# A graph kernel on one core: which engine's queue carries the stores of running sums in layers 2 and 3

## The reference, cut to what matters

```
for l in range(3):                       # gated graph layers
    m   = x @ weight[l]
    agg = segment_sum(m[src] * edge_weight[:, None], dst, 6250)
    x   = gru_cell(agg, x, ...)
x = layernorm(x0 + x)
for W, b in ...:                         # three more layers
    x = relu((x + segment_sum(x[src], dst, 6250)) @ W.T + b)
x = layernorm(x1 + x)
```

## Time and profile before

| what | value |
|---|---|
| median of 3 runs | 2888.23 us (2887.8 to 2888.54) |
| the profiled execution's own time | 2885.88 us |
| its span, first to last instruction | 2884.1 us |
| granted TensorE clock, mean | 0.993 |
| PE busy | 2832.0 us, 98% |
| DVE busy | 1250.6 us, 43% |
| ACT busy | 946.7 us, 33% |
| POOL busy | 887.9 us, 31% |

### The profile page before, as it was taken

One profiled execution on the slowest core, in us unless ns is written; L12 is line 12 of the kernel. 1 busy time (PEld: TensorE's weight loads), 2 busy tenths in 40 slices (PEclk: granted clock), 3 DMA queues, 4 the chain that ended last, 5 costly groups with the idle time before them and its releaser, 6 DMA issues.

```text
span 2884.1 us, 72504 instructions
## 1 busy us (share of the span) xinstructions
PE 2832.0 (98%) x29387; PEld 1880.8 (65%) x29387; DVE 1250.6 (43%) x2716; ACT 946.7 (33%) x1891; POOL 887.9 (31%) x1007
## 2 busy tenths in 40 slices
PE   6899999999999999999999999999999999999998
PEld 5899999999999965555555555555655555555554
DVE  7688888777888514344422344343500010001011
ACT  6677777777777610000001011101400010001111
POOL 4244444444444315454541454544100000000000
PEclk8999999999999999999999999999999999999999
DMA  5666666666662299998996988988488868886884
GB/s 197 244 261 262 245 244 262 261 257 241 252 262 114 96 405 347 341 335 338 356 366 255 343 335 329 360 332 324 150 325 301 310 248 302 308 304 247 318 304 161
DMA packets 134009, 810.64 MB, mean 281 GB/s; under 512 B 17208, under 2 KB 27308, under 8 KB 113948
## 3 DMA queue, kind: packets, MB, share of 16 engines
q1 hardware_dynamic: 111228, 758.32, 68.2%
q0 software_dynamic: 19968, 40.46, 4.3%
q10 hardware_dynamic: 2720, 10.62, 0.9%
HBM read 553.01 MB, written 256.33 MB: 281 GB/s over the span
## 4 chain that ended last, share of the span: by engine, by line
PE 97%; ACT 1%; DVE 1%; DMA 1%; issue 1%; POOL 0%; DVEq 0%; POOLq 0%; ACTq 0%
PE ps L969 31%; PE ps L1165 27%; PE ps L1247 19%; PE ps L1240 11%; PE ps L979 1%; PE ps L980 1%; PE ps L1260 1%; PE ps L1261 1%; PE ps L982 1%; PE ps L981 1%; PE ps L1144 1%; ACT ring L1661 1%; DMA x_keep<-xT 0%; PE ps L1267 0%; PE ps L1266 0%
## 5 line engine op out<-in xcount | busy, mean ns | idle before, releaser
L969 PE MATMUL ps<-ring,Y 128*128 128x448 f32 x2352 | 888.4, 539 | 0.0
L1165 PE MATMUL ps<-ring,Y 128*128 128x448 f16 x4116 | 780.6, 352 | 0.0
L1661 ACT ACTIVATE ring<-ps 128x490 f16<-128x490 f32 (+1 forms) x1344 | 698.1, 653 | 182.8 <-PE ps L1240 175.5
L969 PEld LDWEIGHTS ps<-ring,Y 128*128 128x128 f32 x2352 | 446.4, 190 | 434.8 <-issue 434.8
L1165 PEld LDWEIGHTS ps<-ring,Y 128*128 128x128 f16 x4116 | 402.8, 98 | 373.8
L863 POOL DMA_INDIRECT ring<-y_rows,ring x448 | 431.6, 963 | 518.0 <-PE ps L969 261.8
L1247 PE MATMUL ps<-ring,Y 128*128 (+1 forms) x2744 | 571.8, 360 | 0.4 <-ACT shared L1620 0.4
L1247 PEld LDWEIGHTS ps<-ring,Y 128*128 128x128 f32 x2744 | 504.8, 190 | 8.7 <-ACT shared L1620 0.8
L1240 PEld LDWEIGHTS ps<-shared 64*128 64x128 bf16 x18816 | 320.0, 93 | 83.5 <-issue 65.4
L1240 PE MATMUL ps<-shared 64*128 64x49 bf16 (+1 forms) x18816 | 345.6, 189 | 24.2 <-DVE shared L2142 15.5
L1824 DVE TENSOR_SCALAR ring<-ring 128x128 f32<-128x128 f32 x446 | 130.6, 293 | 389.5 <-DMA ring<-y_rows,ring 254.2
(11 more groups left out here) (196 smaller groups left out, 1449.6 us busy)
## 6 DMA issues: line engine op xcount, KB each, us to landing
ring<-adj_w SPq DMA_DIRECT2D x72, 2688.0 KB, 11.9
ring<-adj_h SPq DMA_DIRECT2D x42, 2800.0 KB, 9.4
ring<-adj_h SPq DMA_DIRECT2D x42, 2688.0 KB, 9.3
adj_w<-ring SPq DMA_DIRECT2D x48, 2016.0 KB, 11.8
adj_h<-ring SPq DMA_DIRECT2D x56, 1372.0 KB, 5.0
ring<-adj_w SPq DMA_DIRECT2D x24, 2912.0 KB, 10.3
adj_w<-ring SPq DMA_DIRECT2D x48, 728.0 KB, 6.8
sum_rows<-ring SPq DMA_DIRECT2D x62, 448.0 KB
```

The source lines that it names most:

```text
L969: mm = pe.matmul(ps[:, bank, 0:GW], Y[:, h, :], slab(s)[:, :, h - h0, :], start=(h == 0), stop=(last and h == TILES - 1))
L1165: mm = pe.matmul(ps[:, par, 0:GW], part[:, h, :], counts_slab(par, s)[:, :, h - h0, :], start=(h == 0 and part is Y_high), stop=(h == TILE ...
L1661: act.activation(strip[:, :, c0:c0 + UNIT * WIN].rearrange("p h (d j) -> p d h j", d=WIN)[:, :, :, w0:w1], psum_unit(a)[:, :, kind, :, :]. ...
```

## The change

Stores 0 to 30 leave SyncE's stream; SyncE issues slabs only. GpSimd issues store b after the gather of round 7b + 12, that is, the sixth gather after the store's own last round, once `s_acc` shows that the seven rounds are summed. Store 31 stays where it was, but counts on the same semaphore as the others (`s_last` goes away), and the counts that DVE and GpSimd wait for are changed to match.

```
+STORE_LAG = 5
...
-            def store_sums(layer, b):
-                sp.wait_ge(s_acc, RUN * layer + STORE * (b + 1))
-                sp.dma_start(sums_kept(b), sums_made(b)).then_inc(s_stored[b % 2], 16)
...
                     for s in range(SLABS):
                         dense_slab(layer, g, s)
-                        if g or layer:
-                            for b in sums_due(SLABS * (g - 1 if g else DENSE - 1) + s):
-                                store_sums(layer if g else layer - 1, b)
...
                         stream_counts(0, 0, r, s)
-                        for b in sums_due(SLABS * (DENSE - 1) + HALVES * r + s):
-                            store_sums(N_LAYERS - 2, b)
...
                         .then_inc(s_row[i % ROW_BUFS], 16)
+                    if i % STORE == STORE_LAG and i > STORE:
+                        store_sums(layer, i // STORE - 1)
+
+            def store_sums(layer, b):
+                pool.wait_ge(s_acc, RUN * layer + STORE * (b + 1))
+                pool.dma_start(sums_kept(b), sums_made(b)).then_inc(s_stored[b % 2], 16)
 
             def fetch_ends(layer):
-                pool.wait_ge(s_acc, RUN * (layer + 1))
-                pool.dma_start(sums_kept(STORES - 1), sums_made(STORES - 1)).then_inc(s_last, 16)
-                pool.wait_ge(s_last, 16 * (layer + 1))
+                store_sums(layer, STORES - 1)
                 for half in range(2):
-                    pool.wait_ge(s_stored[half], 16 * (STORES // 2 - half) * (layer + 1))
+                    pool.wait_ge(s_stored[half], 16 * STORES // 2 * (layer + 1))
...
-                        dve.wait_ge(s_stored[half], 16 * ((STORES // 2 - half) * layer + store // 2))
+                        dve.wait_ge(s_stored[half], 16 * (STORES // 2 * layer + store // 2))
```

More of the change, by code:

```diff
@@ L351, in gnn_program @@
         s_ends = [sem(f"s_ends{i}") for i in range(RUN_SPANS)]
-        s_last = sem("s_last")
         s_joined = sem("s_joined")
@@ L550, in dense_slab @@
                 sp.dma_start(slab(s).rearrange("p u h c -> p (u h c)"), group_slab(g, s)).then_inc(s_slab[s], 16)
-            def store_sums(layer, b):
-                sp.wait_ge(s_acc, RUN * layer + STORE * (b + 1))
-                sp.dma_start(sums_kept(b), sums_made(b)).then_inc(s_stored[b % 2], 16)
-            def sums_due(slab_used):
-                return [b for b in range(STORES - 1) if max(PACE_FIRST + PACE_SLABS * STORE * (b + 1) // PACE, 0) == slab_used]
             def dense_streams(layer, first=0):
```

## The result

The changed kernel takes 2895.51 us (2893.17 to 2905.22, 8 runs) against 2888.14 us for the kernel before: ratio 1.0029, 95% interval 1.0019 to 1.0038. It is 0.3% slower where 2889.0 us, no change, was forecast. Its profiled execution took 2894.24 us, span 2892.5 us, 8.4 us more than before.

What follows compares the result with a forecast made beforehand. TensorE was taken to bound the kernel, fully busy in both layers' aggregations, so idle time elsewhere was worth nothing. Terms 0 + 0 + 0 + 0.8 + 0 = +0.8 us on 2888.23 gave 2889.0 us, range 2885.2 to 2896.

Steps and rivals of the forecast that it cites:

- SyncE's stores and DVE's wait: Two terms: slabs asked for up to 4.9 us sooner, and most of DVE's 134.6 us store wait going; each worth 0.
- the wait moved and nothing else: Rival on DVE: the 134.6 us on stores come back as waits on gathers; time as forecast, no chance of its own.
- GpSimd's issue and its wait for rows: GpSimd along each layer: 31 more stores at 0.9 us and a tighter wait, hidden in the pace; worth 0.
- The pace rival: Along both layers: typical landings of 12.2 us make seven rounds outlast the pace, backlog 19 us a layer, 2926 us; chance 0.03.
- The end of a layer: Layer 2's end: store 30 delays round 223 and store 31 by 3.3 us, of which +0.8 arrives; bounds 0 and 10.6.
- slower by the last stores: Rival at round 223's gather: store 30 holds it 7.8 us, +7.8 in layer 2, +5.9 in layer 3, 2901.9 us; chance 0.14.
- Layer 3: Layer 3's end: round 223 and store 31 1.5 us later, less than the 1.94 us before mix 10; worth 0.
- The range: Whole kernel's time: 2885.2 us (all that PE misses) to 2896 us (one layer end paying the last-stores rival's 7.8 us).
- slower: Whole kernel slower by over 0.2% (5.8 us): chance 0.14, from 0.11 for late last stores and 0.03 for pace.

Runs made afterwards that it cites:

- e17: Changed kernel, with TensorE doing the matmuls of layer 2's first flip four times over (24 more): 2896.82 us, ratio 1.0035.
- e11: Changed kernel with STORE_LAG 2 instead of 5, each store behind three further gathers, not six: 2927.71 us, ratio 1.0138.
- e3: Changed kernel, with SyncE loading the residual after layer 3's first four slabs instead of before them: 2888.55 us, ratio 1.0003.
- e13: Changed kernel with the rounds of both layers one slab (10.3 us) earlier: 2887.34 us, ratio 1.0000 to the kernel before.
- e1: Changed kernel again, unedited, as a yardstick: 2896.23 us, ratio 1.0028 to the kernel before.
- e12: Changed kernel again, unedited, as reference on the chip of its runs: 2895.65 us, ratio 1.0029 to the kernel before.
- e5: Changed kernel with only layer 2's stores on GpSimd's queue, layer 3's back on SyncE's: 2897.80 us, ratio 1.0042.
- e18: Kernel before with only layer 2's store 30 moved to GpSimd's queue, plus 24 added matmuls at layer 2's first flip: 2895.05 us, ratio 1.0026.
- e7: Changed kernel with STORE_LAG 6 (store 30 behind round 223) and the residual's load behind layer 3's first four slabs: 2887.74 us, ratio 1.0005.
- e2: Changed kernel with STORE_LAG 6 instead of 5, so store 30 comes behind the gather of round 223: 2890.32 us, ratio 1.0010.
- e16: Kernel before with eight plain transfers of gather size added behind layer 2's end gathers on GpSimd's queue: 2885.81 us, ratio 0.9997.
- e15: Kernel before with eight more gathers behind layer 2's end gathers and the first flip's matmuls repeated 16 times: 2899.05 us, ratio 1.0042.

## Why the prediction was wrong

*SyncE's stores and DVE's wait: 0 and 0.* Right. PE is 456.00 of 456 us busy, DVE's 134.6 us went and the wait for rows rose by 116 us, for nothing. In e17, the changed kernel with added matmuls in a trace of the same kind as that of before, the wait for rows is 396.9 us, against 254.2 + 134.6 = 388.8 for both before: the wait moved and nothing else, as that rival said.

*GpSimd's issue and its wait for rows: 0.* Right, with the condition: at six gathers the waits are 75.3 us over 20, hidden in the pace but for the last; at three (e11) they are 281.9 over 61 and the gap at layer 2's end is 18 us wider. The pace rival's way was right, its point of decision lies further off.

*The end of a layer: +0.8 us.* This is the step that failed, and twice.

First its size. I let store 30 hold round 223 back by 0.9 + 2.4 us. The 2.4 us were the landing of a store beside the residual's load less that of end gathers issued ten microseconds later, beside other loads. Measured: 0.6 us of issue and 14.3 - 9.1 = 5.2 us of landing, 5.8 in all. The residual's load, which the prediction mentions beside rows 8, has no term in its sum. SyncE issues it 3 us before GpSimd issues store 30:

```profile
1473.43 0.33 SPq L618 DMA_DIRECT2D shared<-x_keep  x1
```

e3 and e13, which take it away from store 30 and round 223, bring the landing to 8.2 and 7.5 us. The trace's packet records show how: the store has 4 packets of 7168 bytes per engine, which begin 1.2 us apart, each turn holding a packet of 25088 bytes of the residual's load, 0.93 us long; in e3 they begin 0.3 us apart. 4 x 0.93 = 3.7 us is most of the 5.2. The Trainium skill says in "DMA: Bandwidth & Descriptors", "Queues, rings and completion order", that an engine takes turns between its queues and goes on to the next only when a whole packet is done. This trace agrees: each of the store's packets ahead of the gather cost a whole packet of the load.

Second, the absorption. I had 3.3 us shrink to 0.8 because later end gathers would land faster. They were issued 5.9 us late and the gap grew by 5.5 in this trace, by 7.7 and 7.3 in e1 and e12: nothing was absorbed. There was a cliff where I drew a slope. With gathers still under way at the slab's end TensorE's own semaphore comes late (4.03, 5.61, 5.53 us in three traces), it idles, and its clock falls to 0.50 for the gates; or, if the semaphore is in time, the next slab's transfer gets in the way of the last gathers (e5, e17, e18). The rival "slower by the last stores" named the right place; its price for layer 2, 7.8 us, is about what the medians show (7.4 to 8.0 us), and I gave it 0.14.

*Layer 3: 0.* Right in the end: 506.24 us from its first aggregation to its flip in both traces. The delay of 1.5 us that I expected did not come: measured from layer 3's first aggregation, store 31 was issued 0.4 us earlier than before (2010.58 - 1537.18 against 2004.52 - 1530.73), as round 223 took 1 us less there (8.0 against 9.0). The residual's load isn't there in layer 3; why round 223 was quicker was not looked into.

*The range* held the time, by 0.5 us, which is luck: its upper end came from a rival's price and not from the mechanism of the sum. The chance of "slower", 0.14, did not say what the profile had to say: a path with 0.2 us of slack and an uncertain delay on it of 3 to 8 us.

## What to carry to other kernels

A transfer put ahead of the last link of a chain can meet the busiest moment of the other queue, so look up what the other queue issues in the same microseconds, even if that transfer has nothing to do with the change. Where a path has no slack, do not let a delay melt away by averages of landings; ask what happens when the engine behind it really stands still. And before moving a queue's work, find the few of its instructions that are on the path: here it was 1 of 62, and the cure was the start of the whole chain one slab earlier.

## What was not expected of the hardware

The semaphore of TensorE's last slab arrived 1.4 to 10.9 us after its matmuls' end in ten of the twenty traces, at ScalarE and SyncE at once, and only at the layers' ends, with indirect gathers of GpSimd (512 bytes a row, and the completion writes of 4 bytes that the packet records show beside them) shortly before or under way. In two more it was another semaphore of TensorE's, at the same place (the flip's in e5, 2.5 us, and the gates' in e7, 2.2 us). Evictions for which ScalarE was free took 0.04 to 0.32 us everywhere else. The Trainium skill, in "TensorE: Matmul & The Clock Gate", "The cost: per-tile semaphore tail", has a fit of such a tail with 26 ns for each increment beside a fixed 25; that makes, as an estimate, tens of nanoseconds for a single one. It fits the 0.04 us and not the rest; here the measurement decides.

What delays it stays open, and the traces narrow it by three facts. It takes no idle TensorE: in e2's layer 3, in e5 and in e7 it was busy. In nine of the cases the semaphore came 2.8 to 3.2 us after GpSimd had issued its last end gather (in e2's layer 2 at 1519.77, the last issue ending at 1516.75), in the others from 2.2 us before to 4.2 us after. And all twelve traces are among the thirteen that lack semaphore records; the thirteenth, e11, had no end gather out as its slab ended in layer 2. None of the seven full ones has a late semaphore, although before in layer 2 (last issue over at 1515.33, slab's end 1517.51) and e16 in layer 3 (2032.97 and 2033.2) come as near to the last gather with no added matmuls. So what the recording of the profile itself has to do with it is an open rival that I did not test, and the on-time evictions of e15, e17 and e18 don't decide it. The times don't either, as a span and a clock were recorded of every execution. The loss of the change doesn't hang on it: e5, whose eviction was on time, is no faster than the changed kernel. The ends of matmuls are modelled in these traces, so the last write may be what is late and not the increment; that ScalarE and SyncE agree within 0.01 us says only that it isn't on their side.
